# Scatter-add over five tables: the rotation from the first tile on, and the order of the first loads

## The reference, cut to what matters

```
xn    = layernorm(x)
agg   = segment_sum(edge_attr, dst) / max(count(dst), 1)
gnn   = xn + relu([xn, agg] @ W1 + b1) @ W2 + b2
q,k,v = xn @ W_qkv.T + b_qkv, by head; q,k = sigmoid(q), sigmoid(k)
mix   = flow attention over the heads of a token, weights normalised over all tokens
x1    = x + gnn + mix @ W_out.T + b_out
out   = x1 + gate * (layernorm(x1) @ W_expert + b_expert), one expert chosen by the mean over all tokens
```

## Time and profile before

| what | value |
|---|---|
| three runs | 2153.13, 2153.62, 2155.49 us; median 2153.62 |
| profiled execution | 2150.43 us; span 2148.7 us |
| PE busy | 1891.6 us, 88% |
| PE weight loads busy | 1510.3 us, 70% |
| DVE busy | 1218.9 us, 57% |
| ACT busy | 558.0 us, 26% |
| POOL busy | 1361.6 us, 63%, of it the scatters 1313.8 us |
| transfers | 397.47 MB, mean 185 GB/s |

### The profile page before, as it was taken

The page is one execution under the profiler, slowest core; times in us unless marked ns, Lnnn a source line. Parts: engine busy times, 40 slices in busy tenths (PEclk is TensorE's granted clock), DMA queues, the critical chain, the costliest instruction groups (busy, mean ns, idle before and its releaser), DMA issues. The chain is left out here.

```text
span 2148.7 us, 30948 instructions
## 1 busy us (share of the span) xinstructions
PE 1891.6 (88%) x10775; PEld 1510.3 (70%) x10775; DVE 1218.9 (57%) x3855; ACT 558.0 (26%) x1314; POOL 1361.6 (63%) x912
## 2 busy tenths in 40 slices
PE   2899999999999999788767898789745999999798
PEld 2688888888888888444446777667634888887586
DVE  4634335444354342477655676566536888885575
ACT  1422233322333222111131222122212333333210
POOL 3788888888888888888888888888881111011100
PEclk9999999999999999766687999889877999999899
DMA  8777777777777767899799999999847766653884
GB/s 296 190 146 161 146 141 156 156 151 137 160 156 148 147 129 142 207 214 214 173 266 223 180 227 196 219 190 195 152 89 208 229 207 209 202 190 114 286 297 150
DMA packets 515321, 397.47 MB, mean 185 GB/s; under 512 B 348603, under 2 KB 385739, under 8 KB 515166
## 3 DMA queue, kind: packets, MB, share of 16 engines
q1 hardware_dynamic: 385838, 340.83, 54.8%
q0 software_dynamic: 127216, 54.59, 23.9%
q10 hardware_dynamic: 2112, 0.07, 0.1%
HBM read 242.42 MB, written 152.96 MB: 184 GB/s over the span
## 5 line engine op out<-in xcount | busy, mean ns | idle before, releaser
L298 POOL DMA_INDIRECT table<-edge_sums,edge_row x831 | 1313.8, 1581 | 297.5 <-issue 234.1
L242 DVE SCALAR_TENSOR_TENSOR edge_sel<-edge_dst_all,edge_dst_f,upper 128x128 f32<-128x128 int16 x831 | 317.7, 439 | 80.1 <-PE edge_sum L254 71.9
L351 PE MATMUL pr_out_bank<-pr_norm_xT_hi,pr_w_hi 128*128 128x512 f32 (+1 forms) x832 | 329.9, 397 | 0.5 <-ACT pr_stage L741 0.5
L351 PE MATMUL pr_out_bank<-pr_norm_xT_lo,pr_w_hi 128*128 128x512 f32 (+1 forms) x832 | 321.1, 386 | 0.0
L351 PE MATMUL pr_out_bank<-pr_norm_xT_hi,pr_w_lo 128*128 128x512 f32 (+1 forms) x832 | 321.0, 386 | 0.0
L254 PEld LDWEIGHTS edge_sum<-edge_attr,edge_sel 128*128 128x128 f32 x1662 | 229.5, 207 | 98.3 <-DVE edge_sel L242 69.3
L254 PE MATMUL edge_sum<-edge_attr,edge_sel 128*128 128x65 f32 x1662 | 239.5, 292 | 57.6 <-DVE edge_sel L242 57.3
L264 ACT ACTIVATE edge_sums<-edge_sum 128x260 f32<-128x260 f32 (+1 forms) x209 | 80.6, 386 | 612.7 <-PE edge_sum L254 559.6
L2090 POOL DMA_DIRECT2D x_rows<-gn_x x49 | 26.7, 545 | 272.7 <-DVE gn_x L2005 258.0
L351 PEld LDWEIGHTS pr_out_bank<-pr_norm_xT_lo,pr_w_hi 128*128 128x128 f32 x832 | 156.5, 188 | 34.8
L351 PEld LDWEIGHTS pr_out_bank<-pr_norm_xT_hi,pr_w_hi 128*128 128x128 f32 x832 | 156.9, 189 | 30.8 <-ACT pr_stage L741 1.0
(11 more groups left out here) (201 smaller groups left out, 3260.9 us busy)
## 6 DMA issues: line engine op xcount, KB each, us to landing
edge_dst_all<-dst SPq DMA_DIRECT2D x103, 256.0 KB
edge_attr<-in_edge_attr SPq DMA_DIRECT2D x103, 256.0 KB
qk_T<-pr_stage SPq DMA_DIRECT2D x48, 512.0 KB, 3.4
h_pre_T<-pr_stage SPq DMA_DIRECT2D x48, 512.0 KB, 3.3
gn_pre<-h_pre_T SPq DMA_DIRECT2D x12, 2048.0 KB, 10.4
done<-qk_T SPq DMA_DIRECT2D x16, 1024.0 KB, 5.5
table<-edge_sums,edge_row POOLq DMA_INDIRECT x831
pr_norm_x<-in_x SPq DMA_DIRECT2D x12, 1024.0 KB, 8.6
```

The costliest lines, as they stand in the source:

```text
L242: op = dve.scalar_tensor_tensor(out=self.sel[q][0:rows, j, 0:rows], in0=self.dst_all[k][0:rows, t:t + m * (rows - 1) + 1:m], scalar=self.d ...
L298: pool.indirect_dma_start(self.c.table[t], bass.IndirectOffsetOnAxis(ap=self.row[k][0:rows, j:j + 1], axis=0), self.sums[k][0:rows, j, :], ...
L351: mm = pe.matmul(out, a, c, start=first and i == 0, stop=last and i == n - 1)
```

## The change

Three edits. `table_of` gives each tile its table by the tile's number modulo five, from the first tile on; before, the first four tiles alternated between two tables, and the eight after them went over three. Each table has a semaphore of its own for its zeros; before, tables 3 and 4 shared one. And SP issues the zeros of tables 3 and 4 before x of block 0 instead of after it, so the zeros of all five tables stand ahead of x of block 0 and of the weights.

```diff
 def table_of(tile):
-    return tile % (2 if tile < 4 else 3 if tile < 12 else TABLES)
+    return tile % TABLES
...
-        added, tables_zero = sem("added"), [sem(f"tables_zero{i}") for i in range(4)]
+        added, tables_zero = sem("added"), [sem(f"tables_zero{t}") for t in range(TABLES)]
...
-    ZERO_AT = (0, 1, 2, 3, 3)
...
     def zero_table(sp, t):
         sp.dma_start(c.table[t].rearrange("(p b a) c -> p b (a c)", p=P, b=2),
                      zero[:, :].unsqueeze(1).to_broadcast([P, 2, TROWS // P * ECOLS // 2])
-                     ).then_inc(tables_zero[ZERO_AT[t]], 16)
+                     ).then_inc(tables_zero[t], 16)
...
         edges.load(sp, 1, 1)
-        norm.load(sp, 0, 0, BT)
         zero_table(sp, 3)
         zero_table(sp, 4)
+        norm.load(sp, 0, 0, BT)
         edges.load(sp, 2, 2)
         weights.load(sp, 0, 2)
...
     def zeroed(pool, t):
-        pool.wait_ge(tables_zero[ZERO_AT[t]], 16 * ZERO_AT.count(ZERO_AT[t]))
+        pool.wait_ge(tables_zero[t], 16)
```

## The result

The changed kernel is slower: 2162.34 us (median of 16 runs, 2157.33 to 2165.46) against 2155.03 (16 runs, 2149.13 to 2158.79); ratio 1.0029, 95% interval 1.0021 to 1.0037, which is +6.2 us (4.5 to 8.0); the two medians differ by 7.3 us. The forecast was +8.0 and 2161.6. The profiled execution took 2157.33 us with a span of 2155.6, 6.9 us more than that of before.

What follows compares the result with a forecast made beforehand. It took PE's start of block 0, PE's gapless work and POOL's last 375 scatters as the bound. x's delay +8.5, less 0.3 and 0.2, gave +8.0 us on the 2153.62 median: 2161.6 us, range 2156 to 2165.

Steps and rivals of the forecast that it cites:

- What bounds the front: Up to the last scatter: PE's start of block 0, then PE's work, then POOL's last 375 scatters set the time.
- The prediction's last term, the 375 scatters: From 899.6 to 1618 POOL runs 375 scatters to the front's end, 718.4 us, 1.916 each.
- x lands with the last of its set: First loads: x of block 0 lands last, at 43.2, delaying DVE's statistics by 8.5 us, bounds 6.3 and 11.1.
- The small terms: Between DVE's statistics and PE's start of block 0: two savings, -0.3 and -0.2 us, off the 8.5 us delay.
- -0.3 for the table load: ACT's square root in block 0 no longer waits for a table load, done long before x arrives: -0.3 us.
- The -0.2 for the edge sum: PE's first edge sum inside block 0 no longer waits for a selection held by edges of batch 3: -0.2 us.
- The rotation at 0: POOL's early scatters over five tables: tile 12 at 54.7 instead of 69.45, 14.7 us gained, worth 0 at the end.
- no lead of POOL: At 196.99 and 899.70 POOL's scatters waited for rows, so production, not POOL's own past, set their time.
- POOL's gain arriving: Rival: the scatter chain is the only clock, so the early waits come off the end; -14.7 us, 2138.9; chance 0.05.
- x hardly later: Rival: on the load queue x passes or shares time with the zeros; +0.5 to +3.5 us, about 2155.6; chance 0.10.
- The phase of the last 375 scatters: Rival: scatters meet the attention part's loads differently, 6 us either way; bad case 2166 and above, chance 0.05.
- The 435 GB/s of the Trainium skill: Alternative load rate: x of block 0 at 40.6, a delay of 5.9 and a sum of 5.4 us instead of 8.0.

Runs made afterwards that it cites:

- the half dose: Changed kernel with only table 3's zeros ahead of x of block 0, table 4's behind it; 2156.55 us, ratio 1.0003 to the kernel before.
- the larger dose: Changed kernel with x of block 0 also behind the edges of batch 2 and half the QKV weights; ratio 1.0063 to the kernel before.
- the rotation alone: Changed kernel with x of block 0 back ahead of the zeros of tables 3 and 4; 2158.47 us, ratio 1.0006 to the kernel before.
- the early x: Loads reordered so x of block 0 comes earlier than in the kernel before; with that kernel's table rule 2158.23 us, ratio 1.0013 to it.

## Why the prediction was right

*What bounds the front.* Right for the changed kernel; for the kernel before it holds in one profile of four, as said below. In the eight profiles in which POOL found no rows ready at tile 80 (and PE had no stall), tile 456 came 837.2 to 839.4 us after PE's first product, with PE's start anywhere between 57 and 76 us. In four others (840.6, 841.2, 842.0, 847.9) there was no wait for rows at tiles 80 and 456: POOL's own pace. The fourth execution of the kernel before stands between (839.3), and 849.0 is PE's stall. The prediction's last term, the 375 scatters that it takes as POOL's own pace, is not quite that: in the kernel before POOL is idle for longer than normal once more at tile 676:

```profile
1321.53 1.54 POOL L298 DMA_INDIRECT table<-edge_sums,edge_row  x1 [1.15 <-issue]
```

In all 14 profiles every idle stretch above 0.42 us in these 375 that the profile puts down to "issue" stands before the first tile of a quad, where POOL waits for rows and sums. So the production touches POOL in this stretch too.

*x lands with the last of its set.* Right in kind, in the first profile a little too late in size: 41.88 in place of 43.2 (43.26 in the second execution), so a delay of 7.2 where I had 8.5. The queue runs first in, first out as far as this shows; the half dose and the larger dose moved x by what was put before it.

*The small terms.* -0.3 for the table load was right: the square root now starts at 44.91, right behind its input (statistics at 41.88, root 3.0 later, against 3.4 before), and the gap from statistics to PE is 26.37 instead of 26.65 us. (It is 26.31 to 26.42 in four of the five profiles in which DVE waits for x, 26.73 in the fifth, the second execution of the changed kernel, and 26.65 to 27.05 in the nine others.) The -0.2 for the edge sum can't be told apart.

*The rotation at 0.* On POOL itself it was sized well: table 4 took its first scatter at 40.36 (forecast 39.6), tile 12 came at 55.50 (54.7). Its worth on the path is the step that was only half right. In the profile I worked from, POOL ran dry at tiles 80 and 456, and I read this as no lead of POOL. It was hardly any lag of PE either: the waits there were 0.24 and 0.43 us above the normal 0.30, and in all three further executions POOL waited for nothing beyond 0.3 us from tile 12 to tile 456 and reached it 1.1, 2.4 and 3.7 us later than in the first. So in part of the executions of the kernel before, the change takes POOL's delay away and adds PE's. The means of tile 456 are 901.5 for four executions of the kernel before and 907.4 for two of the changed one: +5.9, near the measured +6.2 (4.5 to 8.0), where the first profiles alone give 7.6. That this is why the measured loss is smaller than 8.0 fits these profiles, but it isn't shown, and one run speaks against it: the rotation alone should then have gained 1 to 2 us, 0.9995 or less, and was timed at 1.0006 (0.9997 to 1.0015).

*The number.* That 2161.6 lies within 0.8 us of 2162.34 is in part luck. The forecast added 8.0 to 2153.62, the median of three runs; the median of 16 is 2155.03. The difference itself came out at 6.2 us, with the 8.0 at the upper end of its interval.

*The rivals.* POOL's gain arriving: refuted by the rotation alone. x hardly later: refuted by 8.09 us of waiting. The phase of the last 375 scatters: the spread is real, 711.7 to 722.6 us, but it lies between single executions (714.9 to 722.4 in four of the kernel before); the two of the changed kernel (714.4, 718.7) show no shift. The 435 GB/s of the Trainium skill (DMA: Bandwidth & Descriptors, Where 436 GB/s comes from) would have put x at 40.6. It came at 41.88 and 43.26, 42.6 in the mean, so the trace's own step of 4.55 us a table was the nearer one by the mean; the first execution alone lies midway.

## What to carry to other kernels

A wait that the page lists at the start of a chain is worth nothing if the chain later waits for someone else; look for the last place at which it ran dry, and ask how near to dry it was. Where two limits stand within a few microseconds, one profile can't say which is the bound, and a gain needs both moved: here the table rule and the early x were worth nothing or a loss alone and 3.4 us together. On a full load queue every transfer put ahead costs its own time to whoever waits behind it, so order the first loads by when they are needed, all of them: the version that left one load of 0.5 MB behind had PE wait 6.7 us, and fall back by 9.

## What the runs showed of the hardware

A few indirect issues on POOL take 3 to 4.7 us instead of 1.55. Early on they come between 47 and 97 us, at another tile in each version, often two in a row (4.65 and 2.98; 3.38 and 2.98). Later each of the 14 profiles has one of 4.5 us between 1123 and 1149, in half of them with another of 3 to 3.7 right before it. What causes them was not tried.

375 scatters with the same instructions before and after them took between 711.7 and 722.6 us. That is nearly as much as the spread of the runs of one kernel, 2149.57 to 2161.99 us in 29 runs of the kernel before.

PE's first products of block 0 start 0.43 us apart and the later ones 0.23, in every profile, though the granted clock of the kernel before reads 1.00 from 62 to 64 (6 products) as from 68 to 70 (10). Where the pace changes differs from one execution to the next, and with it the time from PE's start to its second group of edge sums: 13.39 us with the larger dose, 14.39 in the changed kernel. That 1.0 is about half of what t456-PE differs by in these two, 837.2 and 839.1. The cause stays open.
